# A fused cross-attention kernel: its prologue reordered, and identity products between TensorE's products

## The reference, cut to what matters

```python
# layer 0: 16 heads of 16, with MLP
q = layer_norm(x, ln1_w, ln1_b) @ q_w + q_b
k = ctx @ k_w + k_b
v = ctx @ v_w + v_b
hidden = softmax(where(mask, q @ k.T / 4, min)) @ v @ cproj_w + cproj_b + x
x = hidden + gelu(layer_norm(hidden, ln2_w, ln2_b) @ fc_w + fc_b) @ proj_w + proj_b
# layer 1: one head of 256
s = (x @ w_q.T) @ (ctx @ w_k.T).T / 16
x = x + alpha * softmax(s) @ (ctx @ w_v.T) @ w_o.T
```

## Time and profile before

| what | value |
|---|---|
| time, median of 3 runs (lowest, highest) | 336.18 us (334.94, 336.44) |
| the profiled execution: its time, its span | 335.6 us, 333.8 us |
| mean granted clock of TensorE | 0.938 |
| TensorE busy | 276.5 us, 83% |
| VectorE busy | 218.8 us, 66% |
| ScalarE busy | 189.9 us, 57% |
| GpSimd busy | 90.4 us, 27% |

### The profile page before, as it was taken

The page is one execution under the profiler, slowest core; times in us unless marked ns, Lnnn a source line. Parts: engine busy times, 40 slices in busy tenths (PEclk is TensorE's granted clock), DMA queues, the critical chain, the costliest instruction groups (busy, mean ns, idle before and its releaser), DMA issues.

```text
span 333.8 us, 5436 instructions
## 1 busy us (share of the span) xinstructions
PE 276.5 (83%) x2065; PEld 199.4 (60%) x2065; DVE 218.8 (66%) x430; ACT 189.9 (57%) x352; POOL 90.4 (27%) x87
## 2 busy tenths in 40 slices
PE   3670978987779897999898979998989997859895
PEld 3460426853226575866585758665956776658784
DVE  4550787377485967886758778867378664454854
ACT  3542084369565569596645695966466697315612
POOL 2143000212200138742002387440010354033300
PEclk9995599779589999999999999999999999978999
DMA  5129996007418202900443029004530000000000
GB/s 186 24 59 138 169 264 211 2 21 115 111 31 112 97 0 66 178 5 0 95 50 128 1 57 119 3 0 93 54 127 0 2 2 0 2 1 0 2 31 31
DMA packets 21489, 21.59 MB, mean 65 GB/s; under 512 B 2388, under 2 KB 18856, under 8 KB 21464
## 3 DMA queue, kind: packets, MB, share of 16 engines
q1 hardware_dynamic: 20168, 18.11, 28.8%
q10 hardware_dynamic: 1296, 3.15, 2.6%
HBM read 10.50 MB, written 1.05 MB: 35 GB/s over the span
## 4 chain that ended last, share of the span: by engine, by line
PE 46%; DVE 24%; ACT 12%; issue 5%; DMA 5%; SPq 4%; POOL 4%; ACTq 0%; DVEq 0%
DVE neg_max L1284 8%; PE post_ps L501 8%; PE om L573 6%; PE pre_ps L488 6%; PE s L546 5%; PE post_ps L505 4%; PE s L563 4%; DMA k_stack<-kp 3%; SPq L419 2%; ACT q_stack L977 2%; SPq L427 2%; PE s L501 2%; DVE ft L1367 1%; ACT probs L986 1%; PE post_ps L835 1%
## 5 line engine op out<-in xcount | busy, mean ns | idle before, releaser
L1284 DVE TENSOR_REDUCE neg_max<-s 128x1 f32<-128x512 f32 x128 | 83.4, 683 | 26.7 <-PE s L546 25.8
L986 ACT ACTIVATE probs<-s 128x512 f32<-128x512 f32 x128 | 75.5, 599 | 28.0 <-PE s L563 27.5
L546 PE MATMUL s<-k_stack,q_stack 97*128 97x512 bf16 x128 | 49.7, 414 | 21.5 <-DMA k_stack<-kp 14.9
L563 PE MATMUL s<-q_stack,k_stack 109*128 109x256 bf16 x256 | 50.6, 281 | 2.5 <-ACT q_stack L977 1.7
L546 PEld LDWEIGHTS s<-k_stack,q_stack 97*128 97x128 bf16 x128 | 12.4, 99 | 47.2 <-DVE neg_max L1284 21.8
L573 PE MATMUL om<-probs,vals 128*17 128x256 f32 x512 | 35.4, 397 | 0.0
L563 PEld LDWEIGHTS s<-q_stack,k_stack 109*128 109x128 bf16 x256 | 20.9, 101 | 16.6 <-ACT q_stack L977 3.6
L1615 POOL TENSOR_TENSOR ln<-ln,minus_half 128x2 f32<-128x2 f32 x8 | 5.6, 703 | 86.9 <-DVE ln L1248 86.9
L977 ACT ACTIVATE q_stack<-om 13x1024 bf16<-13x1024 bf16 x16 | 16.3, 1017 | 13.7 <-PE om L553 13.3
L573 PEld LDWEIGHTS om<-probs,vals 128*17 128x17 f32 x512 | 12.1, 99 | 14.0 <-issue 7.3
L1310 DVE TENSOR_TENSOR y_l<-post_ps,y_h 128x512 fp32r<-128x512 f32 x12 | 8.3, 689 | 16.3 <-ACT y_h L1000 16.3
(11 more groups left out here) (315 smaller groups left out, 715.1 us busy)
## 6 DMA issues: line engine op xcount, KB each, us to landing
k_stack<-kp SPq DMA_DIRECT2D x48, 128.0 KB
q_stack<-qp SPq DMA_DIRECT2D x48, 64.0 KB
cx<-in_ctx_dram SPq DMA_DIRECT2D x4, 512.0 KB, 6.0
pcx<-in_ctx_dram ACTq DMA_DIRECT2D x3, 512.0 KB, 3.6
xz<-in_x_dram SPq DMA_DIRECT2D x5, 256.0 KB, 5.7
raw_late<-in_L_xattn_fc_w_dram SPq DMA_DIRECT2D x1, 1024.0 KB, 12.3
raw_late<-in_L_xattn_proj_w_dram SPq DMA_DIRECT2D x1, 1024.0 KB, 12.1
h<-in_x_dram ACTq DMA_DIRECT2D x3, 256.0 KB, 2.6
```

What stands on the lines that cost most here:

```text
L546: pe.matmul(s1[:, s % 2, :], q_stack[0:ROW_MAX, hd, chunk(t)], k_stack[0:ROW_MAX, hd, :], start=True, stop=True).then_inc(s1_full, 1)
L563: mm = pe.matmul(s2[:, s % 2, i * LQ:(i + 1) * LQ], k_stack[:, hd, chunk(k)], q_stack[:, hd, :], start=True, stop=True)
L986: act.activation(probs[:, g % 2, s // 2, k:k + 2, :], s2[:, s % 2, :].rearrange("p (k n) -> p k n", k=2), ACT.Exp).then_inc(s2_free, 1)
L1284: dve.tensor_reduce(neg_max[:, g % 2, s % 2, s // 2:s // 2 + 1], s1[:, s % 2, :], AX.X, ALU.max, negate=True).then_inc(s1_free, 1)
```

## The change

- SyncE's prologue sends x and context as before, then the two biases directly into one column per half, in head order (`bk`, the new `qb`), then the weights of WA, then `stack_heads(0, 0)`. The maxima's selection rows, the other layer-1 weights and `cproj_w` follow, then `stack_heads(0, 1)`, and only then `load_pre(1)`.
- ScalarE issues the vectors, `k_w`, `q_w`, the mask and `v_w`.
- For batch 0's first half, the keys' copies go ahead of the queries', and TensorE makes the first key projection before the query projection (`FIRST_ORDER`). VectorE writes the high part of the key weights, GpSimd their low part.
- VectorE subtracts the parts of q and of the first half of k; GpSimd keeps the second half's.
- The query's bias row goes over ScalarE and two small products; the key's needs none.
- TensorE makes 7 + 4 + 8 products identity times identity (`keep_warm`), before the vectors' transpose, before the query bias product and before the first `max_tile`.
- WA moves from slot 8 into the prologue. WT, WO, WC, CB and the splits of `fc_w` and `proj_w` move to later slots, with WO ahead of CB.
- Counts of semaphores follow.

```diff
+FIRST_ORDER = (U_CT, U_CT + 1, U_ZT, U_K, U_Q, U_K + 1, U_V, U_V + 1)
-EARLY_AT = {7: U_CT, 8: U_CT + 1, 9: U_ZT, 10: U_Q, 14: U_K, 22: U_K + 1}
+EARLY_AT = {7: 0, 8: 1, 9: 2, 11: 3, 14: 4, 22: 5}
-PREP_AT = {8: "WA", 10: "WT", 12: "CB", 13: "WO", 14: "WC", 16: "WF0", 18: "WF1", 24: "WP0", 26: "WP1",
-           38: "END"}
-PREP_LOW_AT = {11: "WT", 12: "WA", 13: "CB", 14: "WO", 15: "WC", 22: "WF0", 23: "WF1", 28: "WP1", 30: "WP0"}
+PREP_AT = {16: "WT", 18: "WO", 19: "WC", 21: "CB", 22: "WF0", 24: "WF1", 28: "WP0", 30: "WP1", 38: "END"}
+PREP_LOW_AT = {17: "WT", 19: "WO", 21: "WC", 22: "CB", 24: "WF0", 26: "WF1", 31: "WP0", 36: "WP1"}
 SyncE, stack_heads
+                if b == 0 and c == 0:
+                    keys()
+                    queries()
+                else:
+                    queries()
+                    keys()
 SyncE, prologue
-                sp.dma_start(raw_q, q_w.rearrange("(c p) n -> p c n", p=P)).then_inc(wq_in, 16)
...
+                for dst, v in ((bk, k_b), (qb, q_b)):
+                    for c in range(DC):
+                        sp.dma_start(dst[:, c:c + 1], v[chunk(c)].rearrange("(h d) -> d h", h=HC).unsqueeze(2),
+                                     allow_slow_non_contiguous=True).then_inc(bias_in, 16)
+                for i, w in ((0, l1_q), (1, l1_k)):
+                    sp.dma_start(raw_l1[i], w.rearrange("(p c) n -> p c n", c=DC)).then_inc(wa_in, 16)
+                stack_heads(0, 0)
                 sp.wait_ge(consts, 2)
                 for g in range(NG):
                     sp.dma_start(k_stack[ROW_MAX:ROWS, g * GH:(g + 1) * GH, :], sel[:]).then_inc(sel_in, 16)
-                stack_heads(0, 0)
+                for i, w in ((2, l1_v), (3, l1_o)):
+                    sp.dma_start(raw_l1[i], w.rearrange("(c p) n -> p c n", p=P)).then_inc(wo_in, 16)
+                sp.dma_start(raw_c, cproj_w.rearrange("(c p) n -> p c n", p=P)).then_inc(wc_in, 16)
+                stack_heads(0, 1)
                 load_pre(1)
-                stack_heads(0, 1)
 TensorE, prologue
+            def keep_warm(n):
+                for _ in range(n):
+                    pe.matmul(s2[:, 1, 0:P], ident[:], ident[:], start=True, stop=True)
                 pe.wait_ge(consts, 1)
+                keep_warm(7)
                 pe.wait_ge(vec_in, 16 * 6)
+                pe.transpose(s1[:, 0, 0:VECS], vec_rows[:], ident[0:VECS, 0:VECS]).then_inc(vec_ps, 1)
+                pre(0, U_CT)
+                pre(0, U_CT + 1)
+                pre(0, U_ZT)
+                keep_warm(4)
...
+                pe.wait_ge(wk_lo, 1)
+                pre(0, U_K)
...
                 pe.wait_ge(w_lo, 1)
                 pre(0, U_Q)
+                pre(0, U_K + 1)
+                prepare("WA")
                 pe.wait_ge(w_lo, 2)
                 pre(0, U_V)
+                pe.wait_ge(bq_done, 3)
+                keep_warm(8)
                 for s in range(SLOTS):
                     max_tile(0, 0, s)
 ScalarE, prologue (after its ten DMAs)
+                pre(0, U_CT)
                 act.wait_ge(wq_in, 16)
                 act.wait_ge(vec_done, 2)
                 for k in range(DC):
                     a = act.activation(parts_of(wq[0][:, k, :]), by_head(raw_q[:, k, :]), ACT.Copy, scale=lnq[:, k:k + 1])
...
+                key_high(0, 0)
+                key_middle(0, 0)
+                act.wait_ge(bq_done, 3)
+                pre(0, U_Q)
+                query_middle(0)
 VectorE, prologue
-                dve.memset(q_stack[ROW_MASK:ROWS, :, :], 1.0).then_inc(dve_const, 1)
+                dve.memset(q_stack[ROW_MASK:ROWS, 0:HC, :], 1.0).then_inc(dve_const, 1)
...
+                take_mask(0)
+                dve.wait_ge(bias_in, 64)
+                pre(0, U_K)
...
+                key_rest(0, 0)
+                low_weights(wv[1][:], raw_v, wv[0][:], 2)
+                key_low(0, 0)
+                query_rest(0)
+                dve.memset(om[:], 0.0).then_inc(post_free[0], 1)
+                query_low(0)
+                dve.memset(q_stack[ROW_MASK:ROWS, HC:H, :], 1.0).then_inc(dve_const, 1)
+                pre(0, U_K + 1)
```

More of the change, by code:

```diff
@@ new lines, in keys @@
+                def keys():
+                    await_alone(sp, row_done, b + 1)
+                    sp.dma_start(k_stack[ROW_MASK:ROW_MASK + 1, heads, :],
+                                 mask_row[0:1, :].unsqueeze(1).to_broadcast([1, HC, LK])).then_inc(stacked[c], 16)
+                    made = ((kh_done, 2 * b + c + 1), (km_done, 2 * b + c + 1), (k_parts, 2 * b + c + 1))
+                    for part, (sem_, n) in enumerate(made):
+                        await_alone(sp, sem_, n)
+                        for i in [i for i, p in enumerate(TERMS_K) if p == part]:
+                            sp.dma_start(k_stack[i * HD:(i + 1) * HD, heads, :], kp[:, part, c, :]).then_inc(stacked[c], 16)
@@ L509, in pre @@
             def pre(b, n):
-                await_(pe, pre_free, PRE_USES * b + n if not (isinstance(b, int) and b == 0) else
-                       n - 2 if n < U_Q else max(n - 2, U_ZT + 1))
+                at = pre_place(b, n)
+                await_(pe, pre_free, PRE_USES * b + n if b > 0 else max(at - 2, DC if n == U_K else U_ZT + 1) if n > U_ZT else at - 2)
                 if n == U_ZT:
@@ L1161, in prologue @@
             def prologue():
-                for n in range(U_CT, U_ZT + 1):
-                    pre(0, n)
+                row = 0
+                for v in (ln1_w, ln1_b, v_b, ln2_w, ln2_b, fc_b):
+                    n = v.shape[0] // P
+                    act.dma_start(vec_rows[row:row + n, :], v.rearrange("(r p) -> r p", p=P)).then_inc(vec_in, 16)
+                    row += n
+                act.dma_start(raw_k, k_w.rearrange("(c p) n -> p c n", p=P)).then_inc(wk_in, 16)
+                act.dma_start(raw_q, q_w.rearrange("(c p) n -> p c n", p=P)).then_inc(wq_in, 16)
+                act.dma_start(mask_u[:], mask[0:1, :].partition_broadcast(P)).then_inc(mask_in, 16)
+                act.dma_start(raw_v, v_w.rearrange("(c p) n -> p c n", p=P)).then_inc(wv_in, 16)
+                pre(0, U_CT)
                 act.wait_ge(wq_in, 16)
@@ L1701, in prologue @@
                 rstd(ln1, ln1_step, 0, rstd1)
+                pool.wait_ge(wk_hi, 1)
+                for k in range(DC):
+                    i = pool.tensor_tensor(parts_of(wk[1][:, k, :]), by_head(raw_k[:, k, :]),
+                                           parts_of(wk[0][:, k, :]).bitcast(F32), ALU.subtract)
+                i.then_inc(wk_lo, 1)
+                mask_row_of(0)
                 pool.wait_ge(vec_done, 1)
@@ L1705, in prologue @@
                     .then_inc(prep_step, 1)
[L1706 to L1711 removed]
+                key_rest(0, 1)
+                key_low(0, 1)
             def tail(step):
```

185 lines of the change are left out of this document (82 added, 103 removed).

## The result

The changed kernel took 322.55 us (median of 4 runs, 321.18 to 325.27) against 336.31 for the kernel before on the same chip (4 runs): a ratio of 0.961, 95% interval 0.957 to 0.965. The forecast of 324.0 and its range of 318.5 to 331.5 held it. Six more runs of the same kernel later gave 324.01 (319.30 to 325.53), and the ten together have a median of 323.66. Medians and ranges here are of all runs, while the ratios leave out a kernel's runs that lie over 1.5% above its fastest one. The profiled execution took 323.64 with a span of 321.9, against 335.6 and 333.8: 11.9 us less in the span, where the steps sum to 12.2.

A forecast was written before the change was run, and what follows sets the result against it. Bound: the wait ending last in each stage, no engine being busy throughout. Gains 7.2, 9.6 and 0.5 (x's statistics sooner) less losses 1.6, 2.2 and 1.3 give 12.2; 335.6 - 12.2 + 0.6 = 324.0 us, range 318.5 to 331.5.

The forecast's parts named there:

- Landing of the first stacks, 7.2 earlier: Prologue: with keys issued first, the stacks land at 26.1 against 33.3, 7.2 us earlier (5.4 to 8.9).
- Second queue, 0: Prologue: key weights issued from ScalarE's queue leave sooner, but the chain ends on VectorE, so 0 gained.
- splits on VectorE, 0: Prologue: middle and low parts come sooner on VectorE but wait behind a busy queue of copies, so 0 gained.
- identities, a cost of at most 0.5: Prologue: identity products cost at most 0.5 us; their warming of TensorE's clock is worth 0, 1.2 if VectorE is earlier.
- it is hidden at either clock: Prologue: the key product, between 9.9 and 13.2 us, lies beside VectorE's work at either TensorE clock.
- The late context, 1.6 given back: Slot 7 of batch 0: TensorE waits for batch 1's context, landing at 42.2, giving back 1.6 us (0 to 3).
- Preparation out of slots 7 to 16, 9.6 gained: Batch 0 before 72.3 us: WA, CB and WO leave this stretch, gaining 9.6 us (5 to 10.9).
- WO and CB into the next stage, 2.2 lost: Slots 16 to 21: WO and CB make 6.2 us against a 4.0 wait for batch 1's stacks, losing 2.2 (0 to 5).
- The late splits, 1.3 lost: Slots 24 and 26: VectorE makes two low parts of `wf` outside the transfer wait, losing 1.3 us (0 to 2.3).
- Full cover: Rival: CB and WO fit wholly in batch 1's stack wait, later splits in idle VectorE; 320.5 us, chance 0.20.
- Preparation not the bound: Rival, slots 7 to 16: query parts, exponentials and lows become the chain, returning half of 9.6; 330.2 us, chance 0.15.
- the bias gather: Rival, prologue: element-by-element bias copies land near 27 and delay keys; 338.5 us; this or another late transfer, chance 0.10.

The follow-up runs named there:

- experiment 2: Changed kernel with SyncE's old order of copies in the first stack, queries before keys: 326.77 us, ratio 0.974 to the kernel before.
- experiment 6: Changed kernel with all of ScalarE's prologue load issues given to SyncE, so one queue: 323.70 us, ratio 0.962 to the kernel before.
- experiment 5: Changed kernel with the prologue's four subtractions for first keys and queries back on GpSimd: 325.25 us, ratio 0.968 to the kernel before.
- experiment 1: Changed kernel without its 19 identity products: 321.96 us, ratio 0.957 to the kernel before.
- experiment 3: Changed kernel with batch 1's loads issued between the two stacks, as before the change: 320.39 us, ratio 0.951 to the kernel before.
- context and weights early: Changed kernel without identities, with batch 1's x and context plus 1.8 MB of later weights loaded before the first stack: 324.64 us.
- experiment 9: Two kernels, changed kernel without identities, batch 1's context loaded early, WO made in the prologue: 321.10 us; with CB also in four parts: 318.25 us.
- experiment 4: Changed kernel with all preparation but WA back ahead of the 16th exponential tile, WO still ahead of CB: 326.46 us, ratio 0.972.
- context early: Changed kernel without identities, with batch 1's x and context loaded before the first stack: 319.93 us, ratio 0.953 to the kernel before.
- WO in the prologue: Changed kernel without identities, batch 1's x and context, w_v and w_o loaded early, WT and WO made before the first stacks: 321.10 us.

## Why the prediction was right, step by step

*Landing of the first stacks, 7.2 earlier:* 6.75. The chain to the key issue came as laid out (14.16 for 13.9). Of the 8.9 and 3.3 counted behind it, 12.5 were used. The sixth key issue of 1.81 us accounts for what is over: in the four kernels with the keys first, no identities and no more than 1.3 MB loaded early, where that issue is as short as the others, the first score product comes 12.2 us behind the first key issue (12.16 to 12.22), as counted. Sixteen engines at a share of 1.1 to 1.2 moved 114 to 131 GB/s again, in the microseconds 17 to 24. The forecast's bounds do not follow from its own terms: 1.5 and 3.9 for the queries give 9.0 and 6.6, not 8.9 and 5.4. The order of the copies carries 4.3 of the gain (experiment 2).

*Second queue, 0; splits on VectorE, 0; identities, a cost of at most 0.5:* the three parts that the change is named for, and that one might expect most of, measured as counted (experiments 6, 5 and 1). The "worth 0" of the identities' clock rests on a chain that ends on VectorE. What failed here is "it is hidden at either clock": the key product began at 11.02 and not at 9.9, behind eight identity instructions (0.89) and the bias products (1.82), and ended at 12.62 where VectorE was ready for it at 12.54. At the 2.88 us of 1.2 GHz it would have ended at 13.9. So the fast clock did matter, by about 1.3 us; only it came without the identities as well (experiment 1).

*The late context, 1.6 given back:* the forecast's own times give 1.3 (42.2 less 40.9); the wait is 2.12, and over all profiles it cost about 1.5 (experiment 3). What the sum lacked is the clock behind it, at 0.50 until 52. The wait is not its only cause: the kernel before has no such stretch between 43 and 63, but three kernels without that wait (context and weights early, and both of experiment 9) still have 7 us at 0.50 there, while the one-queue kernel, with the longest wait (2.52), has only 3.4 us of it.

*Preparation out of slots 7 to 16, 9.6 gained:* from the second to the third copy the lead grows by 6.8, with all terms (-1.6 + 0.5 + 9.6) at 8.5. The step that was mis-sized is "without them TensorE has 12.7 us of work there": it was busy 14.87, because the first 8 us of the stage ran at 1.2 GHz, where the same work in the kernel before ran at 2.4 until CB. The kernel with one queue has the same 91 instructions of TensorE between the same two points, and its clock came back at 47:

```profile
43.20:56.60 13.40, 12.70 (x91) 7.56 (x92) 9.81 (x19) 8.18 (x17) 2.93 (x4) 0.87 0.45 150
```

It was busy 12.70 us, what was counted, and its stage is 1.9 shorter. So the clock accounts for the missing 1.7. The two kernels differ only in who issues the prologue's loads, so neither case can be read from the order of the work.

*WO and CB into the next stage, 2.2 lost:* 0.7 was lost. From the third copy to batch 1's first score product are 13.25 us before (72.63 to 85.88) and 13.95 after (59.01 to 72.96). The mis-sized term is CB at 4.46: it took 3.46, because the clock stayed at 1.00 through it, and that is 1.0 of the 1.5. This is luck of the profile. In the kernel with the splits on GpSimd CB took 4.68 and the stage to the fourth copy 2.8 us more, which would make some 3.5 lost.

*The late splits, 1.3 lost:* 1.3. From that product to the fifth copy are 10.10 us before and 11.36 after; TensorE's busy time there is the same (8.57 and 8.68), and the part of 1.20 us at 73.34 stands on the chain. From the fifth to the sixth copy 0.2 are gained.

*The rivals.* Full cover (320.5) needed TensorE to be through in the 13.25 us that the kernel before took from the third copy to batch 1's first product; the changed one took 13.95. So its first half came nearly true in this profile, where CB ran fast, and its second half, splits that cost nothing, did not. Preparation not the bound (330.2) is refuted by TensorE's 14.87 of 15.3 and by experiment 4. The slower one, the bias gather, did not come about. The DMA issues of the changed kernel in 0 to 14 us (KB each, us to landing):

```profile
bk<-in_L_xattn_k_b_dram SPq DMA_DIRECT2D x2, 0.5 KB, 3.2
qb<-in_L_xattn_q_b_dram SPq DMA_DIRECT2D x2, 0.5 KB, 4.2
```

Each copy gathers 128 single elements and lands in 3.2 or 4.2 us, before 8, where the key chain needs it at 12.4. The 0.05 us for an element in the forecast came from no row. The Trainium skill's rule in "Rules for kernel authors" of "DMA: Bandwidth & Descriptors", one descriptor per element of such a pattern, is neither shown nor refuted: the 722 packets under 512 bytes that this stretch counts leave room for one for each of the 512 elements. At 128 elements a copy it costs nothing here. Its one visible price is SyncE's 0.65 us for each issue.

So the sum of 12.2 against 11.9 is closer than its terms, and that closeness is luck: 0.4 and 1.7 too much gained in two of them, 1.5 too much lost in a third. The last two have one reason, a clock that was not followed from stage to stage, and they happened to cancel. The way that the gain comes about, keys first and preparation behind the 16th tile, is right. The range's lower end, by its own terms, is 318.7 and not 318.5.

## What to carry to other kernels

Follow a queue backwards from the transfer that ends the wait: the cheapest of all edits here, the order of twelve copies, was worth more than the second queue, the faster engine for the splits and the warming together, none of which shows. Move work from ahead of a point that releases a transfer to behind it, into the transfer's own time, and stop when that time is full. And work a sum for TensorE at both clocks, since the same 91 instructions took 12.7 or 14.9 us here: behind a wait of 1.1 to 2.5 us the clock was low for 3 to 9 us, and it also fell where TensorE was busy throughout. Take such a stretch from the trace where you remove or cause a wait, but as a range and not as a fixed price.

## What the runs showed of the hardware

- The same kernel, on the same chip, took 319.3 to 325.5 us, and its mean granted clock went from 0.961 to 0.941 with it. In profiles of versions that differ little there, the stage from the third to the fourth copy took 14.4 us (changed kernel twice, no identities, context early) or 16.9 to 17.2 (one queue, queries first, splits on GpSimd, context and weights early), with the clock falling within it in the second group; with a shorter stretch at 0.50 it took 15.8 (load between) and 14.9 (WO in the prologue). Of the twelve profiles with CB's 32 one-column products in one piece, the clock fell among them or within 1.1 us behind them in eight, the kernel before among these (4.46 us in the earlier trace rows, with WO behind them at half clock), and not in four; in the two with CB in parts it did not fall in that stage. Spread out between score products, they made the least scattered kernel (0.7 us). That they are the cause is supported by this and not settled, since the four parts alone left a spread.
- Transfers from SBUF into the stacks run at about 120 GB/s with all engines' share full, where the loads of the prologue reached 394 to 414 in their fullest microsecond; that price decides when the first stacks are there.
- One issue of SyncE, the sixth key copy, took 1.81 us instead of 0.60 in the changed kernel. It is always the sixth that is long (1.5 to 1.9). The six took 4.8 to 5.2 us in seven of the profiles after the change and 3.8 to 3.9 in six, among these all five without identity products; the remaining one is the kernel with the queries first, which has them but issues its keys 8 us later. How products on TensorE could lengthen an issue of SyncE no row shows, and it was not tried by itself.
